# LoRA matmuls of tile t-3 placed behind three chunks of tile t instead of two; the first half of y copied out by VectorE, the second by ScalarE, and each PSUM bank waited for by itself

## The reference, cut to what matters

```
logits = x @ Wr.T + 5 * one_hot(language)             # 8 experts
w      = softmax(top_2(logits)); gates = scatter(w)   # 128 x 8 per tile
h      = x @ A.T                                      # 8 experts x 16 ranks = 128 columns
cond   = x @ W.T + 2 * (h * gates) @ B                # LoRA part has rank 128
out    = x + softplus(scale) * (cond @ sign)
```

## Time and profile before

| | before |
|---|---|
| median of three runs | 162.29 us |
| the profiled execution: its time | 162.27 us |
| the profiled execution: its span, first to last instruction | 160.4 us |
| TensorE clock granted | 1.000 of full speed |
| PE / DVE / ACT / POOL busy | 156.9 / 108.0 / 63.8 / 51.8 us |

### The profile page before, as it was taken

The page is one execution under the profiler, slowest core; times in us unless marked ns, Lnnn a source line. Parts: engine busy times, 40 slices in busy tenths (PEclk is TensorE's granted clock), DMA queues, the critical chain, the costliest instruction groups (busy, mean ns, idle before and its releaser), DMA issues.

```text
span 160.4 us, 3654 instructions
## 1 busy us (share of the span) xinstructions
PE 156.9 (98%) x1046; PEld 151.6 (95%) x1046; DVE 108.0 (67%) x451; ACT 63.8 (40%) x178; POOL 51.8 (32%) x50
## 2 busy tenths in 40 slices
PE   8999999999999999999999999999999999999993
PEld 5887899999999999999999999999999999999992
DVE  5899988666656766676666666667666666666651
ACT  3645632244444334334244444433444343334442
POOL 1974535333332313233333333223132333333000
PEclk9999999999999999999999999999999999999999
DMA  5996344324455545444444545545455362222333
GB/s 175 370 161 131 103 129 98 84 71 143 137 140 147 147 142 150 123 135 123 121 124 138 137 139 147 147 143 147 142 148 146 86 186 82 59 70 83 134 130 131
DMA packets 45867, 21.47 MB, mean 134 GB/s; under 512 B 23680, under 2 KB 40864, under 8 KB 45856
## 3 DMA queue, kind: packets, MB, share of 16 engines
q1 hardware_dynamic: 30232, 13.58, 31.0%
q10 hardware_dynamic: 15624, 7.76, 16.8%
HBM read 11.03 MB, written 8.39 MB: 121 GB/s over the span
## 4 chain that ended last, share of the span: by engine, by line
PE 97%; DVE 1%; ACT 1%; issue 0%
PE pair L750 68%; PE pair L786 15%; PE pair L671 3%; PE pair L775 2%; PE pair L691 2%; PE pair L698 2%; PE pair L684 1%; PE pair L731 1%; PE pair L664 1%; PE pair L666 1%; PE pair L665 1%; PE pair L735 1%; DVE ht_lo L580 1%; PE pair L706 0%; PE pair L710 0%; ACT ht_hi L429 0%
## 5 line engine op out<-in xcount | busy, mean ns | idle before, releaser
L327 POOL TENSOR_TENSOR xt_lo<-xt,xt_hi 128x512 fp32r<-128x512 f32 x32 | 41.4, 1293 | 89.8 <-ACT xt_hi L391 86.7
L750 PE MATMUL pair<-wide_hi,xt_lo 128*128 128x392 f32 (+1 forms) x248 | 58.5, 311 | 0.0
L750 PE MATMUL pair<-wide_lo,xt_hi 128*128 128x392 f32 (+1 forms) x248 | 58.4, 312 | 0.0
L750 PE MATMUL pair<-wide_hi,xt_hi 128*128 128x392 f32 (+1 forms) x248 | 58.3, 311 | 0.0
L750 PEld LDWEIGHTS pair<-wide_hi,xt_hi 128*128 128x128 f32 x248 | 38.6, 188 | 0.3 <-issue 0.3
L750 PEld LDWEIGHTS pair<-wide_hi,xt_lo 128*128 128x128 f32 x248 | 38.6, 188 | 0.0
L750 PEld LDWEIGHTS pair<-wide_lo,xt_hi 128*128 128x128 f32 x248 | 38.4, 188 | 0.0
L458 ACT ACTIVATE y<-pair 128x256 f32<-128x256 f32 x31 | 11.9, 385 | 50.9 <-PE pair L786 50.9
L391 ACT ACTIVATE xt_hi<-xt 128x512 fp32r<-128x512 f32 x32 | 20.3, 633 | 7.9 <-DVE xt L499 6.2
L605 DVE TENSOR_TENSOR logits<-pair,bias 128x8 f32<-128x8 f32 x32 | 5.3, 167 | 25.6 <-PE pair L750 25.1
L499 DVE STREAM_TRANSPOSE xt<-x_in 128x512 f32<-128x512 f32 x32 | 22.5, 702 | 0.0
(11 more groups left out here) (105 smaller groups left out, 143.1 us busy)
## 6 DMA issues: line engine op xcount, KB each, us to landing
out<-y SPq DMA_DIRECT2D x31, 256.0 KB, 2.3
x_in<-in_x ACTq DMA_DIRECT2D x104, 64.0 KB, 2.2
h_moved<-h_gated SPq DMA_DIRECT2D x116, 16.0 KB, 1.8
x_in<-in_x SPq DMA_DIRECT2D x24, 64.0 KB, 2.1
w_in<-in_L_cond_W SPq DMA_DIRECT2D x4, 256.0 KB, 4.5
sign_in<-in_L_ffn_sign ACTq DMA_DIRECT2D x3, 256.0 KB, 4.4
sign_in<-in_L_ffn_sign SPq DMA_DIRECT2D x1, 256.0 KB, 5.6
a_in<-in_L_cond_A SPq DMA_DIRECT2D x4, 64.0 KB, 3.9
```

What stands on the lines that cost most here:

```text
L327: nc.gpsimd.tensor_tensor(xt_lo[n][:, :, :].rearrange("p j (g b) -> p g j b", g=NQ), xt[n][:, :, :, :], xt_hi[n][:, :, :].bitcast(FP32).re ...
L750: last = nc.tensor.matmul(pair[n][bank][:, at0:at0 + hi - lo], l[:, k, :], w[:, k, lo:hi], start=(opens and k == 0 and l is xt_hi[n] and w ...
```

## The change

Four things are done:

- In every step of the main part the LoRA of tile s-3 stands behind chunks 0, 1 and 2 of tile s instead of behind chunks 0 and 1.
- VectorE copies the first half of y of tiles 0 to 26, as the last instruction of its step; ScalarE copies only the second half of these. Of tiles 27 to 30 ScalarE copies both halves as before, and raises `late_first_copied` instead of `y_first_copied`.
- TensorE opens bank 0 of a tile when the first half is copied, and bank 1 (the second matmul of the tile) when the second half is.
- SP's store of a tile waits for both halves.

`finish` keeps its order; of its waits one is for the new semaphore.

```diff
-            def store(q, r, d):
+            def store(q, r, d, s):
                 sp_eng.wait_ge(y_copied, RING * q + r + d + 1)
+                if s is None or s + d < LATE - 2:
+                    sp_eng.wait_ge(y_first_copied, RING * q + r + d + 1)
...
-                    if s != TILES - 1 + LAG:
+                    if s is not None and TILES - 2 <= s < TILES - 1 + LAG:
                         nc.scalar.activation(y[n][:, 0:Y0], pair[n][0][:, HEAD:HEAD + Y0], ACT.Copy)\
-                            .then_inc(y_first_copied, 1)
+                            .then_inc(late_first_copied, 1)
                     nc.scalar.activation(y[n][:, Y0:D], pair[n][1][:, 0:D - Y0], ACT.Copy).then_inc(y_copied, 1)
...
+                if s is None or LAG <= s < TILES - 2:       # VectorE, at the end of its step
+                    o = slot(r, -LAG)
+                    dve.wait_ge(y_summed, done - LAG + 1)
+                    if s is None or s - LAG >= RING:
+                        dve.wait_ge(y_stored[o], 16 * turn(q, r, -LAG))
+                    nc.vector.tensor_copy(y[o][:, 0:Y0], pair[o][0][:, HEAD:HEAD + Y0]).then_inc(y_first_copied, 1)
...
                         for bank, lo, hi in cols:           # in wide
+                            if second_after is not None and k == 0 and bank == 1 and w is wide_hi and l is xt_hi[n]:
+                                pe.wait_ge(y_copied, second_after)
...
                     if s is None or s >= RING:
-                        pe.wait_ge(y_copied, done - RING + 1)
+                        pe.wait_ge(y_first_copied, done - RING + 1)
...
-                    wide(r, range(KC // 2), BANKS, opens=True, low_after_high=(s == 1))
+                    wide(r, range(KC - 1), BANKS, opens=True, low_after_high=(s == 1),
+                         second_after=(done - RING + 1 if s is None or s >= RING else None))
                 if has(s, -LAG):
                     pe.wait_ge(ht_lo_made, done - LAG + 1)
                     lora(slot(r, -LAG), (0, 1)).then_inc(y_summed, 1)
                 if s != 0 and has(s, 0):
-                    wide(r, range(KC // 2, KC), BANKS, signals=True)
+                    wide(r, [KC - 1], BANKS, signals=True)
...
-                pe.wait_ge(y_first_copied, s - RING + 1)    # in finish, before the last tile's bank 0
+                pe.wait_ge(late_first_copied, 1)
```

More of the change, by code:

```diff
@@ L200, in adaln_ffn_kernel @@
         y_first_copied = sem("y_first_copied")
+        late_first_copied = sem("late_first_copied")
         last_summed = sem("last_summed")
@@ L286, in turnover @@
                 if s is None or s >= LAG + LEAD:
-                    store(q, r, -LAG - LEAD)
+                    store(q, r, -LAG - LEAD, s)
             for s in range(LAG + LEAD):
@@ L737, in _, with wide @@
             last.then_inc(b2_summed, 1)
-            def wide(r, chunks, cols, opens=False, signals=False, low_after_high=False):
+            def wide(r, chunks, cols, opens=False, signals=False, low_after_high=False, second_after=None):
                 n = slot(r)
```

## The result

The changed kernel takes 163.94 us (median of five runs, 163.57 to 164.90), the kernel before 162.29 us. The ratio is 1.0091, 95% interval 1.0061 to 1.0121: slower by 0.9%. That lies inside the range of the prediction (161.7 to 164.2), but 1.0 us above its figure of 162.9, and among the cases to which it gave 0.35, not 0.61. The profiled execution took 163.92 us, its span is 162.1 us, the granted clock 1.000.

The account below looks back on a forecast made before the run. TensorE, busy 156.9 of 160.4 us, was taken to bound the kernel, so only its gaps could be saved. The sum was 162.27 - 0.63 + 0.98 + 0.32 = 162.94 us, predicted as 162.9, range 161.7 to 164.2.

Parts of the forecast that it names:

- the cases to which it gave 0.35, not 0.61: Whole kernel: slower by over 0.5% had chance 0.35; a change within 0.5% had 0.61.
- the likeliest case: Whole kernel: time changes by no more than 0.5% (0.8 us), about what a measurement can tell; chance 0.61.
- The two-step loop: Main part: LoRA end, ScalarE, GpSimd, VectorE, back to TensorE takes 8.675 us against 8.60; +0.98 us over 26 steps.
- The end: In finish: late GpSimd makes tile 27's ht_lo end 0.35 us later, delaying its LoRA; +0.32 us.
- -0.63 us for the removed stalls: Main part: LoRA one chunk later removes all four long LoRA pieces' excess over 0.72 us; -0.63 us.
- they have more room than before: ScalarE's queue: four load issues ahead of its copy, which comes 0.90 us later, cost nothing.
- The split wait therefore costs nothing: TensorE's opening of banks 0 and 1: ScalarE's second half is done in time, so waiting per bank costs 0.
- its 0.22 us for TensorE's wake: Opening of bank 0: from the copy's end to where TensorE would have been, 0.145 + 0.075 = 0.22 us.
- Rival 1: Main part: copy done in time, loop stays within 8.60 us; 161.96 us, or 161.65 without the end's loss; chance 0.28.
- Rival 2: Opening of bank 0: VectorE's late copy decides each step, loop 8.8 us or more; 164.6 us at 8.80; chance 0.25.
- The border given for that rival: Main part: Rival 2 decides from a loop of 8.70 us on, where time passes 163.1 us (0.05 a step, +1.3).
- Rival 3: GpSimd does not fall on ht_lo, h_gated ends 0.35 us earlier, no loss in loop or end; 161.65 us; chance 0.07.

Follow-up runs that it names:

- x9: Changed kernel without the loads of x for tiles 4 to 31 (issues and transfers left out); 163.08 us, ratio 1.0021 to the kernel before.
- x10: Kernel before without the loads of x for tiles 4 to 31 (issues and transfers left out); 161.79 us, ratio 0.9948 to the kernel before.
- x12: Changed kernel with VectorE's copy made as two instructions of 128 columns; 165.33 us, ratio 1.0158 to the kernel before.
- x5: Changed kernel with GpSimd's xt_lo waiting for the ht_lo of the next step; 164.92 us, ratio 1.0159 to the kernel before.
- x4: Changed kernel with ScalarE's xt_hi put ahead of its wait for the LoRA and its copy; 162.56 us, ratio 0.9986 to the kernel before.
- x11: Changed kernel with TensorE waiting for both copied halves before bank 0; 163.56 us, ratio 1.0071 to the kernel before.
- x1: Kernel before with GpSimd's xt_lo waiting for the same step's ht_lo, already done by then; 162.51 us, ratio 0.9981 to the kernel before.
- x6: Kernel before with GpSimd's xt_lo waiting for the ht_lo of the next step; 162.38 us, ratio 1.0000 to the kernel before.
- x8: Kernel before with only the LoRA moved behind three chunks, ScalarE still copying both halves; 167.08 us, ratio 1.0279 to the kernel before.
- x3: Changed kernel with the LoRA put back behind two chunks, the split copy and separate bank waits kept; 162.32 us, ratio 0.9986 to the kernel before.

## Why the prediction was right and where it was wrong

The range held and the mechanism of the loss was right. The figure was 1.0 us low, and the likeliest case, a change too small to measure, did not come.

*The two-step loop: right in its path and nearly in each term.* Predicted 8.675 us for two steps, 4.3375 for one. Measured: 4.340 over tiles 13 to 23, and 1.02 us between x9 and x10 over the main part, where the sum had 0.98. That it is a loop over two steps is shown by x12 and x5 (half of what is added comes back a step). That it passes ScalarE's order is shown by x4. That it passes GpSimd's hold is shown less directly: x5 took the hold off `ht_lo` and it sprang to the cast, and in x4 `ht_lo` is free and the alternation gone. The terms as read: `xt_lo` 0.71 us behind `xt_hi`, `ht_lo` 0.24 to 0.26 behind `xt_lo`, the copy 0.09 before the end of `h_gated`, 0.416 us long (median of 27; the one copy before took 0.425). The agreement to the third digit is luck. In the changed kernel and in x9 two quiet steps take 8.64 to 8.67 us where no turn of the hardware loop begins, up to 0.03 less than predicted. Where a turn begins, ScalarE's copy starts 0.12 us behind the LoRA's end and not 0.04, and the pair of steps behind that takes 8.70 to 8.75. The prediction had no such term; it makes up for the rest.

The Trainium skill's estimate of 392 ns for this copy, "VectorE: DVE Perf Modes", section on the TRN2 errata, is 6% under the measured median of 416 ns; the loop by it (8.64) would give 4.32, not 4.34.

*The end: right.* Predicted +0.32 from the `ht_lo` of tile 27 held in `finish`. The changed kernel's chain of waits shows it, 0.74 us long, and a LoRA of 0.98 behind it:

```profile
148.41 0.74 DVE ht_lo L583
149.16 0.04 issue
149.20 0.98 PE pair L798 x6
```

x9 less x10 is 0.36 at the end, changed less before 0.41.

*The step that failed: -0.63 us for the removed stalls.* The LoRA's stalls are gone, but not their time. I explained them by GpSimd coming late and did not ask why it came late in four steps of 29. x10 and ScalarE's timeline answer: it is ScalarE's four load issues. Without the loads the kernel before has no late LoRA, and its main part is 116.10 instead of 116.71, just the 0.61 us. The prediction put those issues at nothing, since "they have more room than before". They do, before the copy: four ordinary issues, which made the late LoRAs of the kernel before, are covered in the changed one. But in the changed kernel a single issue sometimes takes 1.5 us, more than that room, and the slack behind the copy had been used up. In the changed kernel one such step reads, on ScalarE:

```profile
56.74 2.73 ACTq L419 DMA_DIRECT2D x_in<-in_x  x3
59.57 0.38 ACT L463 ACTIVATE y<-pair 128x256 f32<-128x256 f32 x1 [3.02 <-PE pair L798]
59.85 0.62 ACT L394 ACTIVATE xt_hi<-xt 128x512 fp32r<-128x512 f32 x1
```

and the chain of waits one step on ends in the opening of bank 0. It does not know of GpSimd's hold: it shows the wait of `xt` (L502) for a held `ht_lo`, which took 1.06 us there, as "issue" ahead of these rows:

```profile
62.00 0.68 DVE xt L502
...
63.99 0.43 DVE y L658
64.42 0.14 issue
64.56 1.60 PE pair L762 x9
```

With the loads the changed kernel's main part is 117.80 - 117.12 = 0.68 us longer than without, that of the kernel before 0.61. The term should have been 0.68 - 0.61 = +0.07, not -0.63. With that the sum is 162.27 + 0.07 + 0.98 + 0.32 = 163.64, against 163.92 of the profiled execution; 0.20 us of the rest arises ahead of the first changed step, and 0.09 at the end.

*The wait for each bank by itself:* "The split wait therefore costs nothing" was wrong by x11's profile. It costs 0.024 us a step, 0.6 us over 26 steps, over half of the loop's loss. The sum did not suffer, since its 0.22 us for TensorE's wake, taken from `finish`, where nothing waits for a second bank, happened to fit the opening with the second wait: again luck.

*The rivals.* Rival 1 (the cover holds) is out. Rival 2 had the right place and side, but its mechanism, a copy that starts late or a loop of 8.8 us, did not occur: the loop is 8.68 on average. The time passed 163.1 for another reason. (The border given for that rival was a slip: by the prediction's own terms a loop of 8.70 gives 163.3, not 163.1.) Rival 3 is what x4 builds on purpose, and it gives 4.290 us a step; it came to 162.56 and not to 161.65; its three long steps each follow on a slow issue (1.54, 0.89 and 1.55 us).

What stays open: why single DMA issues take 1.5 us. They come at about the same places in most profiles (near 39, 57, 126 and 143 us), on SP's queue as well, and in x9 and x10 too, which have no loads: there SP's issues of `h_moved` take up to 1.5 and 1.6 us. ScalarE's are mild in the kernel before (0.86 us at most) and in x1 and x6 (1.11 and 1.18), and reach 1.4 us or more in every kernel with the change and its loads, and in x8 (1.60); no run here says why. Whether the changed kernel with x11's wait and x4's order would be faster was not run either. No complete version ran that beats the kernel before beyond its measurement: x1, x3, x4 and x6 are level with it.

## What to carry to other kernels

An engine that sets the end at 98% busy has a prize no larger than its gaps; before spending the slack of the engines around it, add up how much of that slack already absorbs jitter, here DMA issues on a compute engine's queue. Follow the release of each shared buffer once around, through every in-order queue it passes: the length of that loop over the number of steps in it is the pace. And ask of a stall that occurs in 4 steps of 29 what is different in those four, before counting on its end. Where a loop is too long by hundredths of a microsecond, price every wait on it, also one whose signal comes early.

## What the runs showed of the hardware

- While GpSimd ran its two-input `tensor_tensor` of 128x512 fp32 (1.29 us), some VectorE instructions ended only behind it. `ht_lo` (two SBUF inputs, 0.39 us free) took 0.73 us in the changed kernel's quiet steps and 1.12 in the longest of x3, and ended 0.23 to 0.26 us behind GpSimd. A cast of 128x2 from SBUF to SBUF (0.17 us free) took 0.70 in x5 and ended 0.03 behind GpSimd. The block transposes under it kept their times: 128x128 in 0.31 us (changed kernel, 90.86), 128x512 in 0.71 (x5, 83.72). So the size of a held instruction says nothing of its loss: the two-element cast lost 0.53 us.
- A DMA issue on ScalarE's queue took 0.42 us at the median and 0.86 at most in the kernel before, 0.36 at the median and up to 1.59 in the changed kernel (ns min/median/max):

```profile
L419 ACTq DMA_DIRECT2D x_in<-in_x x104: 317/358/1592, 23.0 to 131.8; - x104
```

- TensorE, held at a wait for a copy, started 0.14 to 0.15 us after the copy's end in the changed kernel and in x11, and 0.15 in `finish` of the kernel before.
